# Query blocks over 128 partitions, zero outside their group, in a sixteen-head cross attention

## What is computed

```python
q = query.reshape(b, sq, h, d)            # h = 16 heads, d = 16
kv = key_value.reshape(b, skv, h, d)
qh = jnp.einsum('bshd,hed->bshe', q, wq) + bq
kh = jnp.einsum('bthd,hed->bthe', kv, wk) + bk
vh = jnp.einsum('bthd,hed->bthe', kv, wv) + bv
scores = jnp.einsum('bshd,bthd->bhst', qh, kh) / jnp.sqrt(d)
attn = jax.nn.softmax(scores, axis=-1)
ctx = jnp.einsum('bhst,bthd->bshd', attn, vh)
return ctx.reshape(b, sq, e) @ wo.T + bo
```

## Time and profile before

| | |
|---|---|
| median of 3 runs | 1930.75 us (1928.44 to 1930.96) |
| span of the profiled execution | 1928.1 us |
| TensorE busy (matmul) | 1752.2 us, 91% of the span |
| VectorE busy | 1071.5 us, 56% |
| ScalarE busy | 856.5 us, 44% |
| GpSimd busy | 642.5 us, 33% |
| score products (L578) | 1024 matmul instructions, busy 180.4 us |

### The profile page before, as it was taken

How to read it: one execution, slowest core, us unless ns; L and a number is a source line. 1 busy time by engine, 2 the same in 40 slices (tenths; PEclk the granted TensorE clock), 3 DMA queues, 4 the chain that set the end, 5 groups by cost and what they waited for, 6 DMA issues and landing times. The chain is left out here.

```text
span 1928.1 us, 37634 instructions
## 1 busy us (share of the span) xinstructions
PE 1752.2 (91%) x12680; PEld 1437.5 (75%) x12713; DVE 1071.5 (56%) x3790; ACT 856.5 (44%) x2361; POOL 642.5 (33%) x1186
## 2 busy tenths in 40 slices
PE   3799999999999999999999999973699999999990
PEld 2477777777777777777777777762699999999990
DVE  4567776777677777777776777747111111111115
ACT  0466665666666666666665666631111111111110
POOL 0234433433343334433443443320233333333320
PEclk7899999999999999999999999995799999999995
DMA  9622222233233233222222220006545545545547
GB/s 309 234 75 83 84 86 80 86 91 89 67 95 91 81 74 92 86 80 83 83 86 80 84 84 18 12 6 236 188 174 183 188 171 185 187 170 187 185 142 267
DMA packets 124351, 235.30 MB, mean 122 GB/s; under 512 B 14448, under 2 KB 76400, under 8 KB 114096
## 3 DMA queue, kind: packets, MB, share of 16 engines
q1 hardware_dynamic: 117392, 214.87, 34.6%
q0 software_dynamic: 6816, 18.62, 2.6%
HBM read 203.16 MB, written 30.28 MB: 121 GB/s over the span
## 5 line engine op out<-in xcount | busy, mean ns | idle before, releaser
L691 ACT ACTIVATE x_prob<-ps,x_nmax 128x257 f32<-128x257 f32 x512 | 238.9, 472 | 228.1 <-DVE x_nmax L992 227.7
L1379 ACT ACTIVATE heT<-ps 128x512 f32<-128x512 f32 x142 | 84.8, 597 | 441.3 <-PE ps L1345 378.1
L1345 PEld LDWEIGHTS ps<-xeT,w_block 128*128 128x128 f32 x2272 | 266.7, 193 | 11.7 <-issue 7.4
L1345 PE MATMUL ps<-xeT,w_block 128*128 128x128 f32 x2272 | 267.3, 276 | 7.5 <-DMA w_block<-in_m_w 7.0
L413 PE MATMUL ps<-context,x_probT 128*128 128x128 f32 x2048 | 272.4, 276 | 0.9 <-ACT x_probT L685 0.8
L413 PEld LDWEIGHTS ps<-context,x_probT 128*128 128x128 f32 x2048 | 256.1, 192 | 9.6 <-DVE x_own L980 1.0
L1331 PE MATMUL ps<-w,heT 128*128 x1136 | 256.8, 379 | 0.0
L1331 PEld LDWEIGHTS ps<-w,heT 128*128 128x128 f32 x1136 | 210.4, 190 | 25.7
L992 DVE TENSOR_REDUCE x_nmax<-ps 128x1 f32<-128x257 f32 x512 | 191.9, 415 | 35.8 <-PE ps L578 35.8
L756 POOL TENSOR_TENSOR x_lastv<-context,x_prob 128x128 f32<-128x128 f32 x256 | 120.1, 469 | 228.9 <-ACT x_prob L691 228.9
L685 ACT ACTIVATE x_probT<-ps 128x512 f32<-128x512 f32 x224 | 133.8, 597 | 124.7 <-PE ps L572 121.8
(11 more groups left out here) (269 smaller groups left out, 3131.9 us busy)
## 6 DMA issues: line engine op xcount, KB each, us to landing
w_block<-in_m_w SPq DMA_DIRECT2D x71, 1024.0 KB
context<-in_cT SPq DMA_DIRECT2D x128, 257.0 KB, 3.0
context<-in_cn SPq DMA_DIRECT2D x128, 256.0 KB, 3.3
context<-in_lastk SPq DMA_DIRECT2D x128, 128.0 KB, 3.6
yrows<-zero SPq DMA_DIRECT2D x1, 8192.0 KB, 28.1
w<-in_m_w SPq DMA_DIRECT2D x8, 1024.0 KB, 11.8
w<-yrows SPq DMA_DIRECT2D x16, 512.0 KB, 6.3
xin<-in_x SPq DMA_DIRECT2D x32, 128.0 KB, 3.3
```

The source lines that it names most:

```text
L691: A(p1[kk % 2][:, g, :], ps[:, g, 0:KEYS], ACT.Exp, bias=nmax1[kk % 2][:, g:g + 1], accum_out=rsum1[kk % 2][:, g:g + 1]).then_inc(e1_ok.ha ...
L1345: t = mm(ps[:, 2 * b + n, f * P:(f + 1) * P], w1[b][:, k, lo:lo + P], xeT[b][:, k, :], start=k == 0, stop=k == H - 1)
L1379: A(heT[b][:, n * FK // 2:(n + 1) * FK // 2, :].rearrange("p k t -> p (k t)"), ps[:, 2 * b + n, :], ACT.Gelu).then_inc(heT_ok.handle, 1)
```

## The change

A query block now has 8 heads x 32 queries = 256 columns on all 128 partitions. Column block g (128 columns) belongs to group g, and its entries are zero on the 64 partitions of the other group. A score product takes 128 partitions and the column block of its group. The sums get 64 zero terms more; the results go to the same places. The multiplication that makes a block (L737) writes 1024 values for each partition and half, not 512. The constant `head_of_dim` has 8 columns, not 4.

```diff
-WIDTH = {..., "head_of_dim": HG, ...
+WIDTH = {..., "head_of_dim": HEADS // H, ...
-    qblk = [sb(f"query_blocks{q}", [P, H, NB, HG, S]) for q in (0, 1)]
+    qblk = [sb(f"query_blocks{q}", [P, H, NB, HEADS // H, S]) for q in (0, 1)]
...
-                mm(ps[:, g, 0:KEYS], qblk[m % 2][g * GD:(g + 1) * GD, k % 2, k // 2, :, :].rearrange("p h q -> p (h q)"),
-                   cT[m][g * GD:(g + 1) * GD, k // 2, k % 2, :], start=True, stop=True).then_inc(s1_ps.handle, 1)
+                mm(ps[:, g, 0:KEYS], qblk[m % 2][:, k % 2, k // 2, g * HG:(g + 1) * HG, :].rearrange("p h q -> p (h q)"),
+                   cT[m][:, k // 2, k % 2, :], start=True, stop=True).then_inc(s1_ps.handle, 1)
...
-                    i = tt(qblk[m % 2][:, h], qT["query1"][:, h, :].rearrange("p (b q) -> p b q", b=NB).unsqueeze(2).broadcast_to([P, NB, HG, S]),
-                           const["head_of_dim"][:].unsqueeze(1).unsqueeze(3).broadcast_to([P, NB, HG, S]), ALU.mult)
+                    i = tt(qblk[m % 2][:, h], qT["query1"][:, h, :].rearrange("p (b q) -> p b q", b=NB).unsqueeze(2).broadcast_to([P, NB, HEADS // H, S]),
+                           const["head_of_dim"][:].unsqueeze(1).unsqueeze(3).broadcast_to([P, NB, HEADS // H, S]), ALU.mult)
...
-    c["head_of_dim"] = (((p % GD) // DH)[:, None] == np.arange(HG)[None, :]).astype(f) * f(DH ** -0.5)
+    c["head_of_dim"] = ((p // DH)[:, None] == np.arange(HEADS // H)[None, :]).astype(f) * f(DH ** -0.5)
```

More of the change, by code:

```diff
@@ L44 @@
 MASKED = -1e30
-WIDTH = {"ident": P, "causal": P, "band": P, "head_of_col": D, "head_of_dim": HG, "fold": S, "before": P,
+WIDTH = {"ident": P, "causal": P, "band": P, "head_of_col": D, "head_of_dim": HEADS // H, "fold": S, "before": P,
          "ones": P, "rev8": EXP, "row": 1, "row_1": 1, "eids": EXP, "cols": P}
```

## The result

The changed kernel takes 1971.7 us (median; 1970.9 to 1972.6), the kernel before 1930.9 us beside it: 1.0219 times as long, 95% interval 1.0205 to 1.0234. The forecast was 1973.2 us. The span of the profiled execution is 1970.7 us, 42.6 us over that of before; the sum had 42.4 us. A total that comes out this near can still be made of wrong parts, and this one was, so most of what follows is about the parts.

What follows compares the result with a forecast made beforehand. The prediction took TensorE to bound the kernel (97% busy): 25.6 us for its score products plus 16.8 us of stall behind unit 7 make 42.4 us over 1930.75, so 1973.2 us; range 1954 to 1988 (8 in 10).

Steps and rivals of the forecast that it cites:

- TensorE bounds the slot; the halves run side by side: TensorE busy 1043 of 1075 us in the main stretch; score products of the two groups share one 0.32 us stretch.
- 0.217 us for each full-array instruction, 0.10 back at a switch and 0.10 for a load: TensorE's score products per unit: four instructions take 0.87 us instead of 0.63, less 0.10 at entry and 0.10 behind.
- Units 3, 5 and 7, the fold behind: +0.12: TensorE where a fold follows the scores: only 0.02 to win behind them, so +0.12 us for each unit.
- The two L737 take 2.0 us each: GpSimd's query-block multiplications: 1.04 us grows to 2.0 each, bounds 1.89 to 2.08.
- L983 in unit 7 stands until the pair ends, plus 0.15: VectorE's step meets GpSimd's second L737 and ends 0.15 us after it, 1.46 us late.
- 0.56 of stall behind unit 7: TensorE waits for late VectorE and ScalarE results: 0.56 us new per slot, 30 slots, 16.8 us.
- No wait later in the slot gives it back: TensorE's two recurring waits follow VectorE steps that move too, so the 0.56 us per slot stays lost.
- unit 1 at 0: TensorE in unit 1: the fold waits for VectorE anyway, so the longer score products add 0 us.
- Rival 1: Only TensorE's own price counts, with no added stall from VectorE: 1956.4 us; chance 0.15.
- Rival 2: GpSimd is slower than twice, an L737 taking 2.4 us: 24 us more, 1997 us; chance 0.15.
- Rival 3: Not slower: VectorE gets ahead and both recurring TensorE waits go, 24.6 us back, 1932 us; chance 0.04.
- Rival 4: TensorE weight loads no longer pass under products, 0.11 us for each of 1024: 2086 us; chance 0.02.

Runs made afterwards that it cites:

- e9: Kernel before, but both groups' score products use the first 64 partitions, so they can't overlap (group 1 left out); 2013.8 us, ratio 1.0437.
- e2: Kernel before with score products over all 128 rows but the old query blocks (groups not separated, result wrong); 1943.5 us, ratio 1.0068.
- e1: Changed kernel with score products back on half of the array, doubled query blocks kept; 1954.5 us, ratio to before 1.0124.
- e3: Changed kernel with GpSimd's L713 for the self attention moved from unit 0 to unit 3; 1959.9 us, ratio to before 1.0152.
- e4: Changed kernel with the query blocks made in four GpSimd steps of 512 values instead of two of 1024; 1946.2 us, ratio to before 1.0083.
- e5: Kernel before plus a GpSimd memset of 2048 zeros per partition behind each tile's two L737; 1931.6 us against 1929.3, ratio 1.0015.
- e6: Kernel before with VectorE's copy of the folded values put ahead of the row maxima in unit 1; 1926.9 us, ratio 0.9989.

## Why the prediction held, and which of its steps did not

- **TensorE bounds the slot; the halves run side by side.** Right. e9 takes the overlap away and loses 83 us. The view of waits of before lists a third wait that comes back, 5.5 us in 31 times, ahead of the feed-forward products of unit 0. It is hardly one: the trace has 96 of these products beside 128 of their loads, so one of each four has no record, and the gap stands where the first would be.
- **0.217 us for each full-array instruction, 0.10 back at a switch and 0.10 for a load.** Right in units 0, 2, 4 and 6 to a hundredth (table, e2).
- **Units 3, 5 and 7, the fold behind: +0.12.** Mis-sized in units 3 and 5. I reckoned the second fold instruction 0.11 after the first, the usual distance; measured it is 0.03 (median 28 ns). In the trace the first fold's load now starts 0.22 us ahead of its product, under the last score; before, it started 2 ns ahead of it. Each costs +0.04. In unit 7 the first load of the scores themselves stands behind a product of 8 columns too short to cover it, which takes 0.08 back, and +0.14 is the measure.
- **Unit 5.** It came out at -0.12 where +0.12 was forecast. Part of it is a cover I had not looked for: before, the start of `a0_wo` is 0.586 us behind the first transpose, after it 0.438. TensorE waited there for 0.15 us between the transposes, and the delay ahead of it used the wait up. With it the second `a0_wo` instruction comes 0.22 behind the first, not 0.30; in e9, where the form is that of before, both are gone too (0.437 and 0.218), so they belong to the wait and not to the form. Of these 0.23 us 0.07 are lost again further on in the unit, and the unit's own price is 0.04, as in unit 3. The view of waits lists this one for two slots only, so I had not counted it.
- **The two L737 take 2.0 us each.** 1.95 and 1.90; the pair took 3.82 instead of 4.0, near the lower end of the bounds. The linear step from 128 and 512 values was the better rule.
- **L983 in unit 7 stands until the pair ends, plus 0.15.** Right: 791.05 against 790.90. It is 1.29 late, not 1.46, by the shorter pair.
- **0.56 of stall behind unit 7.** The place and the mechanism were right (e1: expected 0.71 in all, measured 0.76). In the changed kernel it is 0.51 - 0.14 = 0.37: the maxima are 0.17 less late than forecast. Where it falls was partly wrong: the fold was to wait 0.27 and waits 0.06, and the transposes of the quantised input were to wait 0.05 at most and wait 0.09. In e1, with L983 just as late and TensorE earlier, the fold waits 0.43.
- **"No wait later in the slot gives it back", and unit 1 at 0.** This step failed, in a direction I hadn't considered. I looked only for waits that could shrink, not for other pairs of steps whose order a shift could turn. That L713 holds VectorE too could be read from the trace of before; the earlier trace rows give only the lengths of L822. The 34 `self_norm` steps of L822 that start inside an L713 take 0.80 us or more there, and all others 0.49 or less:

```profile
703.25 0.72 POOL L713 TENSOR_TENSOR self_x_bias<-x,r_a_bv 128x256 f32<-128x256 f32 x1
...
703.32 0.81 DVE L822 TENSOR_SCALAR self_norm<-x,self_moments,self_rstd 128x256 f32<-128x256 f32 x1
```

And unit 1 has L713 0.17 us behind L983. A shift of L983 by 0.13 alone (e2) or of L713 by 0.08 alone (e1) leaves the order as it is; both together turn it and cost 0.43 us a slot (unit 1 at +0.41, against -0.02 in e1 and e2). e3 and e4 each take it away, by different ends.
- **The sum.** TensorE's own price is 0.47 instead of 0.80 (0.33 too much, of which 0.24 in unit 5), the stall in unit 7 0.37 instead of 0.56 (0.19 too much), unit 1 0.43 instead of 0 (too little). 32 x 0.47 = 15 us of forecast 25.6, 30 x (0.37 + 0.43) = 24 of forecast 16.8. That is 10.6 us too much and 7.2 too little, and the remaining 3.5 us of the 42.6 lie outside the full slots, where the forecast had nothing. Errors of opposite sign cancelled: that the total came within 2 us is luck to that extent. e2 and e4 show that the split was wrong where the total was not.
- **Rivals.** Rival 1 (TensorE's price alone, 1956) is not what happened, and e2 shows that it would have been 1943. Rival 2 had no ground. Rival 3 fell: the wait for `x_outT` is 13.9 us as before. Rival 4, by which loads don't pass under products of the same rows, fell in the trace: 0.217 between starts on 128 rows, and e9 shows 0.22 on one half too.

What stays open: the exact reason why GpSimd's L713 starts 0.08 earlier against TensorE in e1 was read only as far as VectorE's step before it (`self_var_eps`, also 0.08 earlier), not tested by a run of its own.

## What to carry to other kernels

Before an array form is changed to "use all rows", look at single starts: if two half-array products start together, no row is idle, and what can be won is only the switches and the loads behind them. Before an instruction of GpSimd that reads SBUF is made longer, look for VectorE steps with two SBUF inputs (or normalising steps like L822) that start just behind its end: here they stood until it was over, and everything in VectorE's queue with them; cutting the instruction in two, at more time in all, gave 25 us here. And with every shift look for neighbouring pairs on two engines whose order is held by a tenth of a microsecond.

## What the runs showed that was not expected

- Two shifts that are harmless alone (0.13 us of L983, 0.08 us of L713) cost 0.43 us a slot together: e1 and e2 have unit 1 at -0.02, the changed kernel at +0.41.
- GpSimd's instruction is held up the same way when VectorE is first: L713 takes 0.84 us in e2 instead of 0.73.
- A GpSimd instruction that only writes SBUF, 1.80 us long, does not delay VectorE's step with two SBUF inputs at all (0.29 us in e5), while one that reads holds it up to 1.58 us (e1).
- Moving 0.57 us of waiting away in one place gave back 0.12 us (e6), and two different edits ended at the same 38.02 us slot.
